# First group of a fused attention and expert kernel: V of group 0 and K of group 1 moved behind the first scores, normalised rows moved ahead of evictions, idle matmuls at the start

## The reference

```python
x = x + attn(layernorm(x), ctx, ctx, mask)        # q = LN(x) @ Wq.T + bq, k = ctx @ Wk.T + bk, v = ctx @ Wv.T + bv
                                                  # softmax(q k^T / sqrt(8), masked) v, then @ Wo.T + bo
x = x + ffn(layernorm(x))                         # router picks one of 8 experts by argmax, gate = its probability
                                                  # y = (relu(LN(.) @ W1[e] + b1[e]) @ W2[e] + b2[e]) * gate
```

## Time and profile before

| what | value |
|---|---|
| median of 3 runs | 333.48 us |
| lowest and highest run | 331.01 and 342.68 us |
| profiled execution, its own time | 330.89 us |
| its span | 329.2 us |
| TensorE busy | 253.6 us, 77% of the span |
| VectorE, ScalarE, GpSimd busy | 222.8, 175.0 and 141.0 us |

### The profile page before, as it was taken

The page is one execution under the profiler, slowest core; times in us unless marked ns, Lnnn a source line. Parts: engine busy times, 40 slices in busy tenths (PEclk is TensorE's granted clock), DMA queues, the critical chain, the costliest instruction groups (busy, mean ns, idle before and its releaser), DMA issues.

```text
span 329.2 us, 8922 instructions
## 1 busy us (share of the span) xinstructions
PE 253.6 (77%) x3112; PEld 200.9 (61%) x3112; DVE 222.8 (68%) x674; ACT 175.0 (53%) x342; POOL 141.0 (43%) x158
## 2 busy tenths in 40 slices
PE   2488999989887879888779576008897989899980
PEld 0335766767565657565667575007786878788880
DVE  6427977887788787677765545723776768677770
ACT  1528786766746584757315311006665756676640
POOL 3812343245473773634713407730443334344442
PEclk9999999999999999999965855556999999999996
DMA  8999999999999700000000001011111211212100
GB/s 233 288 252 212 279 249 206 283 271 288 257 281 291 180 19 11 27 10 2 27 8 10 28 0 34 33 42 44 41 47 45 63 50 43 60 55 65 46 28 0
DMA packets 49611, 36.31 MB, mean 110 GB/s; under 512 B 3087, under 2 KB 45460, under 8 KB 49568
## 3 DMA queue, kind: packets, MB, share of 16 engines
q1 hardware_dynamic: 46864, 31.11, 41.1%
q0 software_dynamic: 2272, 4.27, 4.0%
q10 hardware_dynamic: 432, 0.38, 0.5%
HBM read 14.11 MB, written 22.09 MB: 110 GB/s over the span
## 4 chain that ended last, share of the span: by engine, by line
issue 42%; SPq 30%; DVE 14%; DMA 6%; DVEq 3%; PE 2%; POOL 1%; POOLq 1%
SPq L240 16%; SPq L276 8%; DVE hT L701 4%; DMA out<-ot,G 4%; DVE xh L689 3%; DVE ot L710 3%; SPq L246 2%; DMA G<-rows_dram 2%; DVE yb L708 2%; DVEq L678 2%; SPq L249 2%; SPq L252 1%; PE ps L838 1%; DVE WR L681 1%; DVE VB L483 1%
## 5 line engine op out<-in xcount | busy, mean ns | idle before, releaser
L415 ACT ACTIVATE PT<-ps 128x512 f32<-128x512 f32 x64 | 35.4, 595 | 62.0 <-PE ps L757 59.6
L388 POOL DMA_INDIRECT out<-ot,G x39 | 39.8, 1020 | 65.9 <-DVE ot L710 64.9
L549 DVE TENSOR_REDUCE mx<-ps 128x16 f32<-128x1024 f32 x32 | 39.2, 1225 | 36.5 <-PE ps L733 36.4
L746 PEld LDWEIGHTS ps<-VB,PT 128*64 128x64 f32 x1024 | 35.8, 148 | 17.3 <-issue 17.3
L838 PE MATMUL ps<-xg,WR 128*128 128x128 f32 x312 | 45.3, 290 | 0.0
L746 PE MATMUL ps<-VB,PT 128*64 128x18 f32 x1024 | 38.8, 220 | 4.6 <-ACT OT L408 3.2
L849 PE MATMUL ps<-WR,hT 128*128 128x128 f32 x312 | 41.1, 275 | 0.0
L365 POOL TENSOR_TENSOR Kb<-KT,hmask 128x512 f32<-128x512 f32 x32 | 33.1, 1041 | 18.4 <-PE ps L733 18.1
L838 PEld LDWEIGHTS ps<-xg,WR 128*128 128x128 f32 x312 | 39.4, 198 | 1.4
L419 ACT ACTIVATE Pr<-Pr,rowany 128x1024 f32<-128x1024 f32 x32 | 36.7, 1148 | 5.8 <-DVE Pr L579 5.8
L579 DVE TENSOR_TENSOR Pr<-ps,mx 128x1024 f32<-128x1024 f32 x32 | 39.1, 1221 | 0.3
(11 more groups left out here) (121 smaller groups left out, 387.7 us busy)
## 6 DMA issues: line engine op xcount, KB each, us to landing
rows_dram<-empty SPq DMA_DIRECT2D x32, 528.0 KB, 9.7
WA<-in_wpk SPq DMA_DIRECT2D x8, 578.0 KB
G<-rows_dram SPq DMA_DIRECT2D x39, 66.0 KB, 1.8
X<-in_x SPq DMA_DIRECT2D x8, 256.0 KB, 7.0
C<-in_ctxT SPq DMA_DIRECT2D x8, 256.0 KB, 6.4
XT<-in_xT SPq DMA_DIRECT2D x8, 256.0 KB, 7.3
out<-ot,G POOLq DMA_INDIRECT x39, 2.3
rows_dram<-row,posi POOLq DMA_INDIRECT x32
```

The costliest lines, as they stand in the source:

```text
L388: g.indirect_dma_start(out=out, out_offset=bass.IndirectOffsetOnAxis(ap=G[:, q, D + 1:D + 2].bitcast(I32), axis=0), in_=ot[:, q, :], in_of ...
L415: a.activation(PT[:, p % 2, 512 * m:512 * m + 512], ps[:, 4 + m, :], ACT.Copy).then_inc(freed[4 + m], 1)
L549: v.tensor_reduce(out=mx[:, i % 2, :], in_=psS.rearrange("p g (i k) -> p g i k", k=S), axis=AX.X, op=ALU.max).then_inc(s_mx, 1)
L746: last = mm(psPV[64 * b:64 * b + 64, 18 * j:18 * j + 18], PT[:, p % 2, 128 * j + 64 * b:128 * j + 64 * b + 64], VB[:, p // GP % 3, 2 * (p ...
```

## The change

- `group_ops(step)` takes the place of `group_at` for K, V, transposes of `xn` and Q. It gives the same steps as before, but for two: K of group 1 moves from step -1 to step 0, and V of group 0 from step -4 to step 0. Step 0 then has, behind the scores of pair 0 and all through bank 7: K of group 1, V of group 0, V of group 1 (which was there already).
- On ScalarE the `xn` tile of a step comes ahead of that step's evictions of bank 7, in every step.
- A new tile `idle` (128x512 bfloat16) is cleared by VectorE as its first instruction. TensorE waits for it and then issues 11 matmuls of 512 columns on it, into bank 0, which nobody reads before the scores overwrite it. It issues 9 more ahead of the wait for the first normalised rows.
- The wait for the weights of Q and V moves from V of group 0 to Q of group 0.

```diff
--- before.py
+++ after.py
@@ -38,6 +38,16 @@
         eng.wait_ge(sem, value)
 
 
+def group_ops(step):
+
+    ops = []
+    for name, lead in (("k", 5), ("v", 4), ("xnT", 3), ("q", 2)):
+        for g in range(NG):
+            if step == (0 if (name, g) in (("k", 1), ("v", 0)) else GP * g - lead):
+                ops.append((name, g))
+    return ops
+
+
 def unit_at(step, lag):
 
     u, rest = divmod(step - lag - GP + 1, GP)
@@ -56,9 +66,7 @@
     for i in range(FIRST, LAST):
         if 0 <= i - 2 < NP:
             bank[6].append(("pv", i - 2))
-        for name, lead in (("k", 5), ("v", 4), ("xnT", 3), ("q", 2)):
-            if (g := group_at(i, lead)) is not None:
-                bank[7].append((name, g))
+        bank[7] += group_ops(i)
         if 0 <= i < 3:
             bank[6].append(("weights", i))
         for name, lag in (("onT", 3), ("o0", 4), ("o1", 5), ("r", 10)):
@@ -88,6 +96,7 @@
         Wox, Wo, Wr = Wc[:, 0:OW], Wc[:, OW:OW + D], Wc[:, OW + D:OW + D + E]
         bo_r, br_r = Wc[:, OW + D + E:2 * OW + D + E], Wc[:, 2 * OW + D + E:2 * OW + D + 2 * E]
         Wrc = sb("Wrc", [P, E])
+        idle = sb("idle", [P, 512], BF16)
         bqs = sb("bqs", [P, 1])
         bo_e = sb("bo_e", [P, OW])
         ident = sb("ident", [P, P])
@@ -184,6 +193,7 @@
         s_empty, s_last = sem("empty_row"), sem("last_block_emptied")
         s_fill = [sem(f"rows_emptied{u}") for u in range(4)]
         s_const, s_cdve, s_tab = sem("consts"), sem("dve_consts"), sem("table_steps")
+        s_idle = sem("idle_operand")
         s_bqs, s_pen, s_wrc, s_bo = sem("bqs_ready"), sem("penalty_ready"), sem("router_weights"), sem("output_bias")
         x_in = [sem(f"x_in{g}") for g in range(NG)]
         t_in = [sem(f"xT_in{g}") for g in range(NG)]
@@ -417,11 +427,18 @@
                     act.wait_ge(s_sub, i + 1)
                     wait(act, s_pen, 3 if i == 0 else 0)
                     a.activation(Pr[:, i % 2, :], Pr[:, i % 2, :], ACT.Exp, scale=rowany[:, 0:1]).then_inc(s_p, 1)
-                if (gr := group_at(i, 5)) is not None:
+                for k in range(GP):
+                    if (gr := group_at(i, 7 - k)) is not None:
+                        act.wait_ge(s_nm1, gr + 1)
+                        if gr >= 2:
+                            act.wait_ge(filled[7], nth("xnT", gr - 2))
+                        a.activation(xn[:, gr % 2, k, :], X[:, GP * gr + k, :], ACT.Identity, bias=nm1[:, gr % 2, k:k + 1],
+                                     scale=rs1[:, gr % 2, k:k + 1]).then_inc(s_xn, 1)
+                for gr in (g for name, g in group_ops(i) if name == "k"):
                     act.wait_ge(filled[7], nth("k", gr))
                     wait(act, s_kb, GP * (gr - 1))
                     a.activation(KT[:, gr % 2, :], ps[:, 7, :], ACT.Identity, bias=bk).then_inc(freed[7], 1)
-                if (gr := group_at(i, 4)) is not None:
+                for gr in (g for name, g in group_ops(i) if name == "v"):
                     act.wait_ge(filled[7], nth("v", gr))
                     if gr >= 3:
                         act.wait_ge(filled[6], nth("pv", GP * (gr - 2) - 1))
@@ -430,23 +447,16 @@
                         src = ps[64 * h2:64 * h2 + 64, 7, :].rearrange("k (b j d) -> k b j d", b=2 * GP, d=DK)
                         last = a.activation(VB[64 * h2:64 * h2 + 64, gr % 3, :, :, h2, 0:DK], src, ACT.Copy)
                     last.then_inc(freed[7], 1)
-                if (gr := group_at(i, 3)) is not None:
+                for gr in (g for name, g in group_ops(i) if name == "xnT"):
                     act.wait_ge(filled[7], nth("xnT", gr))
                     if gr >= 1:
                         act.wait_ge(filled[7], nth("q", gr - 1))
                     a.activation(xnT[:], ps[:, 7, :], ACT.Copy).then_inc(freed[7], 1)
-                if (gr := group_at(i, 2)) is not None:
+                for gr in (g for name, g in group_ops(i) if name == "q"):
                     act.wait_ge(filled[7], nth("q", gr))
                     wait(act, s_s, GP * (gr - 1))
                     wait(act, s_bqs, 1 if gr == 0 else 0)
                     a.activation(QT[:, gr % 2, :], ps[:, 7, :], ACT.Identity, bias=bqs[:, 0:1], scale=scale).then_inc(freed[7], 1)
-                for k in range(GP):
-                    if (gr := group_at(i, 7 - k)) is not None:
-                        act.wait_ge(s_nm1, gr + 1)
-                        if gr >= 2:
-                            act.wait_ge(filled[7], nth("xnT", gr - 2))
-                        a.activation(xn[:, gr % 2, k, :], X[:, GP * gr + k, :], ACT.Identity, bias=nm1[:, gr % 2, k:k + 1],
-                                     scale=rs1[:, gr % 2, k:k + 1]).then_inc(s_xn, 1)
                 if (u := unit_at(i, 9)) is not None:
                     act.wait_ge(s_lsub, u + 1)
                     wait(act, s_ls, u)
@@ -480,6 +490,7 @@
         @block.vector
         def _(dve):
             v = nc.vector
+            v.memset(idle[:], 0.0).then_inc(s_idle, 1)
             v.memset(VB[:], 0.0).then_inc(s_cdve, 1)
             dve.wait_ge(s_cdve, 1)
             for h2 in range(2):
@@ -716,6 +727,12 @@
         def _(pe):
             mm = nc.tensor.matmul
 
+            def spin(n):
+                for _ in range(n):
+                    mm(ps[:, 0, :], idle[:, 0:P], idle[:], start=True, stop=True, skip_group_check=True)
+
+            pe.wait_ge(s_idle, 1)
+            spin(11)
             for i in range(FIRST, LAST):
                 if 0 <= i < NP:
                     q, c = i // GP % 2, P * (i % GP)
@@ -757,13 +774,12 @@
                             last = nc.tensor.transpose(ps[:, 4 + m, 128 * j:128 * j + 128],
                                                        Pr[:, p % 2, 128 * (4 * m + j):128 * (4 * m + j) + 128], ident[:])
                         last.then_inc(filled[4 + m], 1)
-                if (gr := group_at(i, 5)) is not None:
+                for gr in (g for name, g in group_ops(i) if name == "k"):
                     pe.wait_ge(c_in[gr], 16)
                     wait(pe, s_wa, 16 if gr == 0 else 0)
                     wait(pe, freed[7], nth("k", gr) - 1)
                     mm(ps[:, 7, :], Wk, C[:, GP * P * gr:GP * P * (gr + 1)], start=True, stop=True).then_inc(filled[7], 1)
-                if (gr := group_at(i, 4)) is not None:
-                    wait(pe, s_wb, 16 if gr == 0 else 0)
+                for gr in (g for name, g in group_ops(i) if name == "v"):
                     wait(pe, freed[7], nth("v", gr) - 1)
                     for b in range(2 * GP):
                         for h2 in range(2):
@@ -772,14 +788,16 @@
                                       Wv.rearrange("p (j t d) -> p j t d", t=2, d=DK)[:, :, h2, :],
                                       start=True, stop=True, skip_group_check=True)
                     last.then_inc(filled[7], 1)
-                if (gr := group_at(i, 3)) is not None:
+                for gr in (g for name, g in group_ops(i) if name == "xnT"):
                     wait(pe, s_const, 5 if gr == 0 else 0)
+                    spin(9 if gr == 0 else 0)
                     pe.wait_ge(s_xn, GP * (gr + 1))
                     wait(pe, freed[7], nth("xnT", gr) - 1)
                     for k in range(GP):
                         last = nc.tensor.transpose(ps[:, 7, P * k:P * k + P], xn[:, gr % 2, k, :], ident[:])
                     last.then_inc(filled[7], 1)
-                if (gr := group_at(i, 2)) is not None:
+                for gr in (g for name, g in group_ops(i) if name == "q"):
+                    wait(pe, s_wb, 16 if gr == 0 else 0)
                     wait(pe, freed[7], nth("q", gr) - 1)
                     mm(ps[:, 7, :], Wq, xnT[:], start=True, stop=True).then_inc(filled[7], 1)
                 if i == 0:
```

## The result

| | before | after |
|---|---|---|
| median (runs) | 332.25 us (4) | 343.19 us (4) |
| lowest and highest | 328.53 and 342.68 us | 341.70 and 346.22 us |
| ratio, 95% interval | | 1.0419, 1.0282 to 1.0556 |
| span of the profiled execution | 329.2 us | 344.3 us |

The ratio compares undisturbed runs alone, which are here the two lowest of the kernel before and all four of the changed one, and so this ratio and those further down are above what the medians give. The forecast was 335.5 us in a range of 331.0 to 339.5. The kernel is slower: the medians lie 3.3% apart, and 343.19 us is outside the range. Beside the later experiments the kernels were run again: 343.75 us (6 runs) against 333.4 (7 runs), ratio 1.0295 with an interval of 1.0166 to 1.0423. The kernel before is spread over more than 10 us in these jobs (329.2 to 345.8 us), the changed one lies between 341.7 and 348.3.

What follows compares the result with a forecast made beforehand. The prediction took attention from 30 us on to be paced by TensorE's instruction stream. 330.89 us profiled plus 3.3 lost at step 0 gave 334.2, or 336.8 with the median's 2.6 excess; it named 335.5, range 331 to 339.5.

Steps and rivals of the forecast that it cites:

- Up to the first scores: Start of the kernel: subtraction of pair 0 ends 6.1 us earlier, 5.7 us after the cost of clearing `idle`.
- The clearing of `idle`: VectorE's first instruction, expected to shift the whole chain of the start by 0.4 us.
- Step 0: Gain handed back behind the first scores: pair 1 0.6 us later at full clock, pair 2 3.3 us later with low clock.
- the term for the low clock: In step 0, half clock after a pause of about 4 us: 2.3 us on top of 0.6 for pair 1.
- The chain of evictions: Step 0, from the end of pair 0's subtraction to pair 1's scores, through ScalarE's bank-7 evictions: 6.4 us.
- a shift of its start should move everything behind it one for one: Attention from 30 us on: paced by TensorE's instructions, its waits summing to at most 5.2 us in 135 us.
- the fall of the clock near the end of attention moves: Rival: pauses shift with the start; a held clock gives 330.2 us, an earlier fall 338; chance 0.05 each way.
- What the 20 idle matmuls cost: At the start, 11 plus 9 matmuls at 0.5 us each, taken to cost the kernel nothing.
- The base: Starting time: 330.89 us of the profiled execution, with the median of three runs 2.6 us above it.

Runs made afterwards that it cites:

- after_again: The changed kernel run once more, with no further edit; 343.75 us (6 runs), ratio 1.0295 to the kernel before.
- after_kept_warm: Changed kernel plus 6 idle matmuls ahead of V of groups 5 to 7 and output projections in steps 27, 28, 31, 32; 338.05 us, ratio 1.0195.
- fill_only: Kernel before plus the fills of after_kept_warm alone, no idle matmuls at the start, `idle` cleared in step 0; 334.19 us, ratio 0.9967.
- xn_first: Kernel before with the `xn` tiles ahead of the bank-7 evictions in every step, nothing else; 338.13 us (10 runs), ratio 1.004.
- after_no_idle: The changed kernel without the idle matmuls at the start; 341.34 us (4 runs), ratio 1.0238 to the kernel before.

## Why the prediction was wrong

- **Up to the first scores: right.** `xnT` 12.85 us (12.6 plus 0.4 forecast), `QT` 14.70, first maximum 16.56 (16.7), end of the subtraction 19.04 (19.2). The clearing of `idle` cost 0.28 us and not 0.4, the idle matmuls 0.39 us each and not 0.5.
- **Step 0: right.** The order exponential, `xn`, `KT`, V, `VB`, V, a pause of 3.73 us (about 4), and the fall in it. Mask term of pair 1 at 26.57, between the 25.5 and 27.3 named (27.61 in after_again, outside); of pair 2 at +2.45 us instead of +3.3 (+3.19 in after_again). Where the two differ it is the term for the low clock: in the first trace the first V took 1.54 us, part of it still warm, in the second 1.89. The chain of evictions, put at 6.4 us, is the 6.6 us that stay with the gap filled.
- **The step that failed** is the one in the first part: "a shift of its start should move everything behind it one for one". It moved everything up to pair 6 one for one (+2.8), and from there it did not: +12.4 us at pair 23. Where no fall of the clock comes between, the step holds (3.1 us at pair 3, 2.8 at pair 31, after_kept_warm against fill_only). TensorE's stream in the loop had pauses of 1.3 to 1.9 us that I had read as a sign of how little slack there was the earlier trace rows; pauses of that kind are also the places behind which the clock can fall. The rival "the fall of the clock near the end of attention moves" had the mechanism, but took one fall near the end, a price of 4 us and 0.05 for an earlier one. It was three falls in the middle, 1.8 to 2.0 us each, and two kinds of longer pauses ahead of them.
- **What the 20 idle matmuls cost** was put at nothing apart from their time. In the first trace a run of V stood at the place where TensorE waits for instructions: 1.7 us at pair 13 and a fall behind it (after_again has the pause, 1.17 us, without the fall). Nothing in the trace of the kernel before showed such a pause, and I named no bound for an effect of added instructions on the instructions behind them.
- **The expert stage** gave 2.6 us of the 15.1. From the first slot's product to the end it took 106.9 us before and 109.5 after; in the profiled executions of all kernels, whose code is the same there, it took 103.8 to 112.8, and 110.3 in fill_only, which has nothing of the change. So it needs no effect of the change, though one trace of each kernel doesn't exclude one.
- **The base.** The median of three runs that I had is one of a distribution that is some 15 us wide; that the two kernels differ is clear, by how much is known only to some 1.3% either way.

What stays open: why `lsub` met GpSimd's work for 3.09 us in this execution, and why, of the fourteen pauses of 1.8 to 1.9 us ahead of the output projection between 100 and 135 us in all traces, eleven were followed by a fall of the clock and three were not, among them the 1.87 us of the kernel before. So why the changed kernel has falls in the middle of attention and the kernel before has none is not settled: it has the same pauses, some of them 0.4 us longer, at other times. What state the gate is in at a pause isn't seen in the profile.

## What to carry to other kernels

A producer that is moved behind a consumer joins another queue: list for each step which instructions share a buffer and on which engine its evictions stand, since two users of one bank in one step wait for whatever that engine has in front. Before trusting that a shift passes through one for one, look at TensorE's pauses. Here those of 1.8 us and more were mostly followed by a fall of the clock and shorter ones seldom, and 1.2 us of idle matmuls in the pause cost less than the fall. Idle matmuls at the start bought 2 us here by pair 3, and the trace that had only them had lost these by pair 13, so judge them by the whole trace. And hold a filled kernel against one that has the fills alone.

## What the runs showed of the hardware

- TensorE paused 0.6 to 2.0 us ahead of matmuls that waited for nothing the profile shows, at fixed places of its instruction stream, 256 instructions or a multiple apart, 1.2 to 1.8 us after a 16 KB packet of the instruction queue had landed (eighteen pauses in twelve traces). With six matmuls added ahead the pause came six matmuls earlier in V.
- A fall of the grant took TensorE to 1.2 GHz for 6.8 us at a time in the changed kernel (3.4 to 17 us in others), and cost attention 1.8 to 2.0 us each. Of ten pauses of 1.3 us ahead of the output projection between 140 and 160 us none had a fall behind it, of ten of 1.7 us between 159 and 176 us one.
- A VectorE subtraction of 32 elements took 0.18 us with no GpSimd tensor operation beside it, and otherwise ended with that operation: after 0.55, 1.3 and, with two in a row, 3.09 us.
- The clearing of 512 bfloat16 ran as 256 words in 0.27 us.
- From one trace to another the expert stage varies with VectorE's wait for gathered rows: 1.1 us where it took 103.8 us (xn_first), 4.3 at 106.9 (before), 8.5 at 111.1 (after_no_idle). In the changed kernel, at 109.5 us:

```profile
DVE xh L700 <- DMA G<-rows_dram: 6.6, 6, 1.5
```
